# A fused attention and feed-forward kernel: one subtraction moved from GpSimd to VectorE, full chunks respaced, and the last numerators divided straight from the bank

## The reference

```
q, k, v = split(x @ Wqkv + bqkv)
q', k'  = exp(q @ omega - |q|^2 / 2), exp(k @ omega - |k|^2 / 2)      # per head, 128 features
num, den = q' @ (k'^T v), q' @ sum_n k'                               # over the 2048 rows of a batch
a  = layernorm(x + (num / (den + 1e-6)) @ Wout + bout)
y  = layernorm(a + a @ W^T + pooled(a) @ disha)
```

## Time and profile before

| | |
|---|---|
| median of 3 runs | 2477.88 us (2476.97 to 2478.51) |
| profiled execution | 2478.22 us, span 2476.1 us, mean granted TensorE clock 0.992 |
| TensorE matmul | 2369.6 us, 96% of the span, 21000 instructions |
| VectorE | 1941.8 us, 78%, 3915 instructions |
| ScalarE | 1276.5 us, 52% |
| GpSimd | 455.0 us, 18% |
| DMA | 213.08 MB, mean 86 GB/s |

### The profile page before, as it was taken

One profiled execution on the slowest core, in us unless ns is written; L12 is line 12 of the kernel. 1 busy time (PEld: TensorE's weight loads), 2 busy tenths in 40 slices (PEclk: granted clock), 3 DMA queues, 4 the chain that ended last, 5 costly groups with the idle time before them and its releaser, 6 DMA issues.

```text
span 2476.1 us, 54866 instructions
## 1 busy us (share of the span) xinstructions
PE 2369.6 (96%) x21000; PEld 1319.0 (53%) x21000; DVE 1941.8 (78%) x3915; ACT 1276.5 (52%) x2313; POOL 455.0 (18%) x514
## 2 busy tenths in 40 slices
PE   8989999999999999999999999999999999997887
PEld 4545555555555555555555555555555555554443
DVE  6768777877878778888777878788877878877876
ACT  4445555555555555555555555555555555554443
POOL 1102221212221212221212221212221112211111
PEclk9999999999999999999999999999999999999988
DMA  6322332332332332332332332332332332331320
GB/s 202 87 73 68 104 91 66 96 95 70 104 94 63 104 88 70 104 91 66 104 89 68 104 95 62 104 87 70 104 95 62 102 89 70 87 78 42 85 74 35
DMA packets 160275, 213.08 MB, mean 86 GB/s; under 512 B 19376, under 2 KB 119824, under 8 KB 156048
## 3 DMA queue, kind: packets, MB, share of 16 engines
q1 hardware_dynamic: 159440, 208.53, 30.3%
q10 hardware_dynamic: 576, 1.05, 0.1%
HBM read 73.19 MB, written 33.55 MB: 43 GB/s over the span
## 4 chain that ended last, share of the span: by engine, by line
PE 79%; DVE 10%; issue 5%; ACT 4%; SPq 1%; DMA 1%; POOL 1%; DVEq 0%; ACTq 0%; POOLq 0%
PE bank_a L450 23%; PE bank_y L450 20%; PE bank_x L450 13%; PE bank_qf L569 5%; PE bank_kf L515 4%; PE bank_x L606 4%; PE kv_ps L541 2%; PE bank_nm L589 2%; DVE k_feat_lo L814 2%; ACT k_feat L674 2%; DVE nm_f L855 1%; PE kv_ps L547 1%; PE bank_a L477 1%; PE bank_x L477 1%; SPq L361 1%
## 5 line engine op out<-in xcount | busy, mean ns | idle before, releaser
L674 ACT ACTIVATE k_feat<-bank_kf 128x512 f32<-128x512 f32 x512 | 305.8, 597 | 241.2 <-PE bank_kf L515 208.4
L814 DVE TENSOR_TENSOR k_feat_lo<-k_feat 128x512 bf16<-128x512 f32 x512 | 375.9, 734 | 52.5 <-ACT k_feat L674 49.6
L684 ACT ACTIVATE q_feat<-bank_qf 128x512 f32<-128x512 f32 x512 | 305.0, 596 | 133.1 <-PE bank_qf L569 123.6
L821 DVE TENSOR_TENSOR q_feat_lo<-q_feat 128x512 bf16<-128x512 f32 x512 | 347.0, 688 | 28.9 <-ACT q_feat L684 26.4
L961 POOL TENSOR_TENSOR rstd<-mean_var,minus_half 128x1 f32<-128x1 f32 x128 | 82.9, 648 | 1289.5 <-DVE mean_var L893 1289.4
L950 POOL TENSOR_TENSOR rows<-rows,bias_out 128x512 f32<-128x512 f32 x128 | 174.9, 1369 | 310.2 <-DMA rows<-x 299.4
L942 POOL TENSOR_TENSOR xt_lo<-xt_f,xt_hi 128x512 f16<-128x512 f32 x124 | 156.0, 1286 | 404.6 <-DVE xt_hi L726 404.6
L700 ACT ACTIVATE at_hi<-bank_x 128x512 f16<-128x512 f32 x112 | 66.9, 597 | 249.6 <-PE bank_x L606 249.5
L777 DVE SCALAR_TENSOR_TENSOR t_lo_k<-bank_a,bias_qk,t_hi_k 128x512 f16<-128x512 f32 x119 | 89.3, 751 | 129.4 <-ACT squares_k L647 129.4
L515 PEld LDWEIGHTS bank_kf<-omega_s,stack_k 98*128 98x128 f16 x1920 | 137.7, 97 | 97.6 <-issue 23.5
L515 PE MATMUL bank_kf<-omega_s,stack_k 98*128 98x128 f16 x1920 | 186.3, 219 | 3.4 <-ACT k_feat L674 3.0
(11 more groups left out here) (196 smaller groups left out, 5237.4 us busy)
## 6 DMA issues: line engine op xcount, KB each, us to landing
rows<-x SPq DMA_DIRECT2D x128, 256.0 KB, 2.9
out<-rows SPq DMA_DIRECT2D x128, 256.0 KB, 2.1
xt_f<-xt SPq DMA_DIRECT2D x31, 1024.0 KB, 5.1
stack_k<-t_hi_k SPq DMA_DIRECT2D x240, 128.0 KB, 2.4
stack_q<-t_hi_q SPq DMA_DIRECT2D x240, 128.0 KB, 2.4
stack_k<-t_lo_k SPq DMA_DIRECT2D x120, 128.0 KB, 2.4
stack_q<-t_lo_q SPq DMA_DIRECT2D x120, 128.0 KB, 2.4
stack_q<-t_hi_k SPq DMA_DIRECT2D x16, 128.0 KB, 2.5
```

Source lines behind the costliest of these rows:

```text
L674: nc.scalar.activation(k_feat[:, i % 2, :], bank_kf[:, :], ACT.Exp, scale=1.0 / WS).then_inc(S["k_exp"], 1)
L684: nc.scalar.activation(q_feat[:, 2 * pair:2 * pair + 2, :], bank_qf[:, :].rearrange("p (e n) -> p e n", e=2), ACT.Exp, scale=1.0 / WS).the ...
L814: v.tensor_tensor(k_feat_lo[:, u, :], k_feat[:, u, :], k_feat_hi[:, u, :], ALU.subtract).then_inc(S["kfl"], 1)
L821: v.tensor_tensor(q_feat_lo[:, at, :], q_feat[:, at, :], q_feat_hi[:, at, :], ALU.subtract).then_inc(S["qfl"], 1)
```

## The change

1. `xt_lo` is no longer made by GpSimd. A new kind of piece, `XL` (0 to 3), makes a quarter of it on VectorE, and stands at four places in every order that has `XS`.
2. In full chunks `AT3'` goes from before `QF0` into the middle of `KP2`, the first half of `QP0` behind `KV11`, `KF0` before the second half of `VP1`, `KF3` behind `QF11`, and `NM4` before the first half of `FF0`.
3. Where `alone` is true, `NM` is three matmuls with 33 columns for all eight heads, all added in the bank; ScalarE's copy and VectorE's addition fall away, and `den` and `attn` read the bank. The bank is free when `attn` is written, not when `nm_f` is.

```diff
@@ ORDER
-WO2' AT3' QF0 KF11' KP2. KV10' KP2 QP0. KF12' KV11' QF1 QP0 WO3'. KV12' QF2 KF13' WO3' YT2' KP3. KF14'
+WO2' QF0 KF11' KP2. KV10' AT3' KP2 KF12' KV11' QP0. QF1 QP0 WO3'. KV12' QF2 KF13' WO3' YT2' KP3. KF14'
...
-QF11 WO1. QF12 YT0 KV2 QF13 WO1 QF14 QP3. KF4 QF15 XS QP3 KV3 VP3. VP3 KV4 FF0. KF5 YT1 NM4 FF0 KV5 KF6
+KF3 WO1. QF12 YT0 KV2 QF13 WO1 QF14 QP3. KF4 QF15 XS QP3 KV3 XL0 VP3. VP3 KV4 NM4 XL1 FF0. KF5 YT1 XL2 FF0 XL3 KV5 KF6
@@ TensorE, NM
-                    wait(pe, "nm_sum", 8 * j + (max(i - 1, 0) if alone(b, c) else i))
+                    if alone(b, c):
+                        wait(pe, "nm_sum", 8 * LAST_Q)
+                        wait(pe, "normed", 8 * j + max(i - 1, 0))
+                    else:
+                        wait(pe, "nm_sum", 8 * j + i)
...
-                        at = WN * hl
-                        width = WN if hl < WIDE else W1
+                        at = W1 * hl if alone(b, c) else WN * hl
+                        width = WN if hl < WIDE and not alone(b, c) else W1
@@ ScalarE
-                elif kind == "NM":
+                elif kind == "NM" and not alone(b, c):
@@ VectorE, NM
+                    if alone(b, c):
+                        sums = units(bank_nm_of(b, c, i))[:, 0:8, :]
+                    else:
+                        sums = nm_f
...
+                elif kind == "XL":
+                    if kA + 1 < B * CPB:
+                        wait(dve, "xt_hi_done", kA + 1)
+                        slot = (c + 1) % CPB
+                        low = v.tensor_tensor(xt_lo[:, slot, i, :], xt_f[:, i, :], xt_hi[:, slot, i, :], ALU.subtract)
+                        if i == KB - 1:
+                            low.then_inc(S["xt_lo_done"], 1)
@@ GpSimd
-                elif kind == "XS":
-                    if kA + 1 < B * CPB:
-                        split_x_low((c + 1) % CPB, kA + 1)
```

More of the change, by code:

```diff
@@ L64 @@
 KP0. KF7' Z0' KP0 QN' KF8' KV6' FF1'. KV7' FF1' AT2' KF9' KV8' KP1. NM6' Z1' KP1 KF10' NM7' WO2'. KV9'
-WO2' AT3' QF0 KF11' KP2. KV10' KP2 QP0. KF12' KV11' QF1 QP0 WO3'. KV12' QF2 KF13' WO3' YT2' KP3. KF14'
+WO2' QF0 KF11' KP2. KV10' AT3' KP2 KF12' KV11' QP0. QF1 QP0 WO3'. KV12' QF2 KF13' WO3' YT2' KP3. KF14'
 QF3 KP3 KV13' QF4 KF15' QP1. KV14' QF5 KN QF6 QP1 FF2'. QF7 KV15' FF2' KFIN0' VP0. YT3' KFIN1' VP0 NM0 QP2. Z2'
-QP2 FF3'. NM1 FF3' VP1. AT0 NM2 Z3' VP1 QF8 KF0 NM3 WO0. KF1 QF9 WO0 KV0 KF2 VP2. AT1 KV1 QF10 VP2 KF3
-QF11 WO1. QF12 YT0 KV2 QF13 WO1 QF14 QP3. KF4 QF15 XS QP3 KV3 VP3. VP3 KV4 FF0. KF5 YT1 NM4 FF0 KV5 KF6
+QP2 FF3'. NM1 FF3' VP1. AT0 NM2 Z3' KF0 VP1 QF8 NM3 WO0. KF1 QF9 WO0 KV0 KF2 VP2. AT1 KV1 QF10 VP2 QF11
+KF3 WO1. QF12 YT0 KV2 QF13 WO1 QF14 QP3. KF4 QF15 XS QP3 KV3 XL0 VP3. VP3 KV4 NM4 XL1 FF0. KF5 YT1 XL2 FF0 XL3 KV5 KF6
 NM5
@@ L72 @@
 ORDER_0 = """
-WV KP0. KP1. KP2. KP3. KP0 KP1 KP2 KP3 VP0. VP0 XS VP1. KN VP1 VP2. VP2 VP3. KF0 VP3 KF1
+WV KP0. KP1. KP2. KP3. KP0 KP1 KP2 KP3 VP0. VP0 XS VP1. KN XL0 VP1 VP2. XL1 VP2 XL2 VP3. XL3 KF0 VP3 KF1
 """
@@ L77 @@
 KP0. KF2' KV0' KP0 KF3' KV1' WQ0 WX0 KP1. KF4' KV2' KP1 KF5' KV3' WF0 KP2. KF6' KV4' KP2 KF7' KV5' WQ1 WX1 KP3.
-KF8' KV6' KP3 KF9' KV7' WF1 VP0. KF10' KV8' VP0 KF11' KV9' KN XS VP1. KF12' KV10' VP1 KF13' KV11' WQ2 WX2 VP2. KF14'
-KV12' VP2 KF15' KV13' WF2 WQ3 WX3 VP3. KF0 KV14' VP3 KF1 KV15' WF3
+KF8' KV6' KP3 KF9' KV7' WF1 VP0. KF10' KV8' VP0 KF11' KV9' KN XS VP1. KF12' KV10' VP1 XL0 KF13' KV11' WQ2 WX2 XL1 VP2. KF14'
+KV12' VP2 XL2 KF15' KV13' WF2 XL3 WQ3 WX3 VP3. KF0 KV14' VP3 KF1 KV15' WF3
 """
@@ L84 @@
 WM QP0. KF10' KV8' QP0 KF11' KV9' KN QP1. KF12' KV10' QP1 KF13' KV11' WE0 VP0. KF14' KV12' VP0 KF15' KV13' WE1 VP1.
-KV14' VP1 KV15' WE2 QP2. QP2 KF0 WE3 VP2. KF1 VP2 KF2 KV0 QP3. KF3 KV1 QP3 KF4 KV2 XS VP3. KF5 KV3 VP3 KF6 KV4 KV5
+KV14' VP1 KV15' WE2 QP2. QP2 KF0 WE3 VP2. KF1 VP2 KF2 KV0 QP3. KF3 KV1 QP3 KF4 KV2 XS XL0 VP3. KF5 XL1 KV3 VP3 XL2 KF6 KV4 XL3 KV5
 """
@@ L146 @@
     "ST0' ST1' LX1 LX0 ST2' ST3' LX3 LX2 STQ NRQ", "XT STK NRK WL"]]
-A_KINDS = ("KP", "VP", "KN", "KF", "KV", "KFIN", "XS", "XT", "STK", "NRK", "WL", "WV", "WQ", "WX", "WF", "WE", "WM")
+A_KINDS = ("KP", "VP", "KN", "KF", "KV", "KFIN", "XS", "XL", "XT", "STK", "NRK", "WL", "WV", "WQ", "WX", "WF", "WE", "WM")
 Q_KINDS = ("QP", "QN", "STQ", "NRQ")
@@ L852, in step @@
                     wait(dve, "nm_done", m)
-                    wait(dve, "nm_low", m)
                     wait(dve, "normed", m - 1)
[L855 to L858, removed]
+                    if alone(b, c):
+                        sums = units(bank_nm_of(b, c, i))[:, 0:8, :]
+                    else:
+                        sums = nm_f
+                        wait(dve, "nm_low", m)
+                        v.tensor_tensor(nm_f[:, :, :], units(bank_nm_of(b, c, i))[:, 0::2, :], nm_l[:, :, :],
+                                        ALU.add).then_inc(S["nm_sum"], 1)
+                        wait(dve, "nm_sum", m)
+                    v.tensor_scalar(den[:, 0, :], sums[:, :, DH:W1].rearrange("p h o -> p (h o)"), DEN_EPS,
                                     None, ALU.add).then_inc(S["den_done"], 1)
@@ L865, in step @@
                     v.tensor_tensor(attn[:, 256 * uu:256 * (uu + 1)].rearrange("p (h d) -> p h d", d=DH),
-                                    nm_f[:, :, 0:DH],
+                                    sums[:, :, 0:DH],
                                     den[:, 1, :].rearrange("p (h o) -> p h o", o=1).to_broadcast([P, 8, DH]),
@@ L937, in _ @@
             pool.wait_ge(S["dve_const"], 5)
[L939 to L944, removed]
             def add_bias(j, t):
```

## The result

The changed kernel takes 2451.77 us (median of 4 runs, 2449.52 to 2453.8), the one before 2477.73: ratio 0.9895, 95% interval 0.9878 to 0.9912. The forecast was 2455. Run once more beside the experiments it took 2450.43 (ratio 0.9896, 0.9877 to 0.9915).

The account below looks back on a forecast made before the run. TensorE was taken to bound the kernel nearly everywhere, so only its waits could pay. Gains of 7.9 (full chunks), 4 (start) and 10.8 us (query-only end) made 22.7, from the median to 2455 us, range 2432 to 2471.

Parts of the forecast that it names:

- The subtraction, on VectorE: Full chunks: four xt_lo pieces fit VectorE's gaps, statistics of FF0 start earlier, AT2 follows half_norm; -0.34 us a chunk.
- Respacing: Full chunks on TensorE: AT3' no longer waits, -0.49 us; waits at KF1 and QF12 go, -0.19 us a chunk.
- GpSimd's additions: Full chunks: last bias addition closes up behind the third, slows a k_feat_lo, QP3. waits for yt_lo; +0.65 us a chunk.
- The rival without a collision: Full chunks: the last bias addition waits for its row's load and delays nothing needed; 2438 us, chance 0.25.
- Full chunks together: All full chunks: -0.37 us for most, -0.38 per pair starting a batch; 7.9 us gained in all.
- The ceiling that I set for them: Full chunks: TensorE's idle time there, some 29 us and a little more by starts, as the most to gain.
- Start: Kernel's start: TensorE's wait for xt_lo halved, -1.65 us, and two KV waits for k_feat_lo gone, -2.3; 4 us gained.
- Query-only end: Last stretch: shorter attn waits 14.6 us, extra matmuls cost 5.8, better clock gives 2; 10.8 us gained.
- The sum: Whole kernel: 7.9 + 4 + 10.8 = 22.7 us gained, giving 2455 us.
- A bank as source: Query-only end: den and attn reading a bank cost nothing extra; by the skill's cycles it would be 4 us more.
- The slower rival: Full chunks: XL pieces delay FF0's statistics and everything behind them; at the bound 2498 us, chance 0.14.

Follow-up runs that it names:

- the kernel with the hold: Changed kernel with the fourth bias addition behind KF6 instead of NM4 in GpSimd's order, full chunks only: 2431.59 us, ratio 0.9821 to the kernel before.
- the two edits alone: Kernel before with only xt_lo moved to VectorE, 2491.7 us; kernel before with only the new order of full chunks, 2484.22 us.

## Why the prediction was right, step by step

- **The subtraction, on VectorE.** Right to the hundredth in the profile: 0.68 each, 4.85 us from `v_both` to the statistics, `AT2` next, held by `half_norm` and 11.67 us behind `v_both` where it was 12.01: the -0.34. What I didn't see is that it depends on the new order: in the old one the gain isn't there. I had put `NM4` into the layout without asking what it does alone.
- **Respacing.** -0.49 and -0.19, 0.68 a chunk; measured alone, 17.9 / 28 = 0.64.
- **GpSimd's additions.** +0.65; the profile has 0.69 at the place shown and 19.2 us idle in 28 waits. Undoing it gave 18 to 20 us in all, 15 to 17 of them in the full chunks, 0.53 to 0.61 a chunk. The mechanism is shown, the size roughly. The rival without a collision is refuted; the kernel with the hold shows what it would have been worth, 2431.6 where I had 2438.
- **Full chunks together.** -7.9; measured -6.3 and, in the second profile, -8.6 (1921.41 us). The ceiling that I set for them, some 29 us and a little more by starts, was too low: by starts the waits were about 53 us, and the kernel with the addition held took 23.5 us out of the stretch.
- **Start.** -4; the waits fell by 4.8 (the one for `xt_lo` and the held `k_feat_lo` among them), but 3 to 7 us at the lower clock came in, so the start was 2.2 us longer in one profile and 1.5 shorter in the other (208.54). All profiles together are the better measure: eight with the subtraction on VectorE took 204.8 to 212.2 us for the start, 208.2 on average, five with it on GpSimd 210.0 to 211.4, 210.5 on average (the first full slot lies mostly in this stretch, and its order isn't the same in all). So the term is about 2.3 and was put too high; half of the wait of 3.04, besides, is 1.52 and not the 1.65 that I wrote. Why the clock differs from one execution to the next isn't explained.
- **Query-only end.** -10.8; measured -20.4 and -18.0. Waits: 14.6 forecast, 14.7 measured. Matmuls: 5.8 forecast, 4.9 measured. So -9.8 where I had -8.8. The clock is the term that was mis-sized: I took 2, and it was 10 and 6 in the two profiles of the changed kernel, but 2.5 with the same end on the kernel before.
- **The sum.** Mechanisms and signs were right in the full chunks and in the waits of the end. That the total came within 3.2 us of 2455 is partly luck: the start gave less than forecast, the end more, and what the clock did in each I had not foreseen.
- **A bank as source.** I put nothing. `attn` takes 424 ns from a bank and took 424 from SBUF, `den` 156 to 167 and 172 (medians). The Trainium skill ("VectorE: DVE Perf Modes", section on the TRN2 errata) has 62 cycles more for a bank; the trace doesn't agree, by the whole 65 ns.

The slower rival, statistics that come late, did not happen in the changed kernel. The step that would have misled on other numbers is the sum itself: it adds a part for each edit, and here the two edits alone cost 14.7 and 7.2 us and give 15.1 together.

## What to carry to other kernels

When work leaves an engine, look at what closes up behind it there: an addition that had been kept apart by the removed work ran into an operation that was needed, and moving that one addition was worth more than the new end alone (18 to 20 and 13.7 us). Before crediting a move, ask what contends with it at the new place; an instruction group moved beside another engine's SBUF work can cost more than the wait that it avoids. And test the parts of a change alone and together, since their gains need not add.

## What the runs showed of the hardware

- Beside GpSimd's operations on SBUF some of VectorE's take longer, and not only those with two inputs in SBUF (`k_feat_lo`, `attn`): `den`, 128x8 with one tile as input, took 0.62 and 1.09 us (0.17 usual). But others with one input in SBUF never did: in the profile before, the row's statistics (128x512) stayed under 0.70 us in all 26 that ran beside a bias addition or a subtraction, and the reciprocal (128x8) under 0.21 in 13. Nor did those with a bank as input: `den` and `attn` on a bank were never over 168 and 426 ns in the 30 executions each shown above. It goes the other way too: GpSimd's power took 0.94 us where 0.55 is usual, when a `k_feat_lo` ran beside it. The Trainium skill ("GPSIMD Engine Reference", section Specifications) names two SBUF inputs or a 2-port mode as the condition; `k_feat_lo` agrees with 1.54 for 0.69, and whether `den` runs in such a mode no run here shows.
- The same code, with the same wait just ahead of it, can run at either clock. TensorE's timeline after, and of the second execution of the same kernel, at the same instructions of the end:

```profile
2386.86 0.39 PE L569 MATMUL bank_qf<-stack_k,omega_s 98*128 98x256 f16 x2 [2.37 <-DMA stack_k<-half_norm]
...
2387.96 0.59 PE L450 MATMUL bank_y<-wout_lo,at_hi 128*128 128x512 f16 x2
...
2392.79 0.63 PE L610 MATMUL kv_ps<-ident,rows 128*128 128x128 f32 x4 [2.06 <-DVE at_lo L879]
2393.25 0.38 PE L569 MATMUL bank_qf<-stack_k,omega_s 98*128 98x256 f16 x2
2394.59 0.39 PE L569 MATMUL bank_qf<-stack_k,omega_s 98*128 98x256 f16 x2 [0.96 <-ACT q_feat L688]
```

```profile
2380.18 0.39 PE L569 MATMUL bank_qf<-stack_k,omega_s 98*128 98x256 f16 x2 [2.12 <-DMA stack_k<-half_norm]
...
2381.50 1.06 PE L450 MATMUL bank_y<-wout_lo,at_hi 128*128 128x512 f16 x2
...
2387.78 1.03 PE L610 MATMUL kv_ps<-ident,rows 128*128 128x128 f32 x4 [2.06 <-DVE at_lo L879]
2388.61 0.64 PE L569 MATMUL bank_qf<-stack_k,omega_s 98*128 98x256 f16 x2
2389.99 0.61 PE L569 MATMUL bank_qf<-stack_k,omega_s 98*128 98x256 f16 x2 [0.75 <-ACT q_feat L688]
```

The idle time ahead is 2.06 us in both, and the transposes take 0.63 and 1.03 us. What lies further ahead is the same code too, but the second execution had fallen to the lower clock there already (two matmuls with 512 columns in 1.06 us, not 0.59) behind a wait of 2.12 us, and recovered in between; the first did not fall behind a longer one, 2.37. What decides it stays open. Between kernels with the same code at the end, the time lost to the lower clock there was 4.9 to 12.4 us, so differences of that size between two such kernels say little.
